# Eight feed-forward projections moved into the last steps of the attention before them, with VectorE as first reader

## The reference, cut to what matters

```python
x = x + tanh(g_xattn[0]) * L0_xattn(ctx_1024, layernorm(x), mask, ...)
x = x + tanh(g_ffn[0]) * L0_ffn(layernorm(x), ...)

def L0_ffn(x):                                  # x: (2048, 128)
    combine = route(x)                          # sigmoid scores of 16 experts in 4 groups,
                                                # best 2 groups, best 4 experts, weights times 2.5
    up = einsum('th,ehi->eti', x, expert_up)    # 16 experts, 64 wide
    down = einsum('eti,eih->eth', silu(up), expert_down)
    moe_out = einsum('te,eth->th', combine, down)
    shared = silu(x @ shared_up) @ shared_down  # 256 wide
    return moe_out + shared
```

## Time and profile before

| | us |
|---|---|
| median of 3 runs (lowest to highest) | 1184.56 (1184.32 to 1186.83) |
| the profiled execution, its own time | 1186.89 |
| its span | 1185.2 |
| TensorE busy (share of the span) | 1099.5 (93%) |
| VectorE busy | 718.4 (61%) |
| ScalarE busy | 706.9 (60%) |
| GpSimd busy | 469.6 (40%) |

### The profile page before, as it was taken

The page is one execution under the profiler, slowest core; times in us unless marked ns, Lnnn a source line. Parts: engine busy times, 40 slices in busy tenths (PEclk is TensorE's granted clock), DMA queues, the critical chain, the costliest instruction groups (busy, mean ns, idle before and its releaser), DMA issues. The chain is left out here.

```text
span 1185.2 us, 22867 instructions
## 1 busy us (share of the span) xinstructions
PE 1099.5 (93%) x8921; PEld 792.8 (67%) x8937; DVE 718.4 (61%) x1385; ACT 706.9 (60%) x1290; POOL 469.6 (40%) x741
## 2 busy tenths in 40 slices
PE   5988898899999999999999889988979988999998
PEld 3554268788888888888887556653546663466667
DVE  6762447555566556656565259984558993645554
ACT  4675530466666666666666468886448986644440
POOL 5771001133422233344444363521484534644441
PEclk8897899899999999999999899998989998999999
DMA  9200000100000000000000200000000000033320
GB/s 334 91 2 1 0 1 2 71 2 1 2 2 1 1 2 1 1 2 1 1 2 1 54 1 2 2 2 0 1 1 1 2 2 1 11 96 103 99 74 19
DMA packets 13884, 29.42 MB, mean 25 GB/s; under 512 B 2737, under 2 KB 5073, under 8 KB 13010
## 3 DMA queue, kind: packets, MB, share of 16 engines
q1 hardware_dynamic: 13778, 27.96, 7.2%
HBM read 25.14 MB, written 1.25 MB: 22 GB/s over the span
## 5 line engine op out<-in xcount | busy, mean ns | idle before, releaser
L1321 POOL TENSOR_TENSOR work<-work 128x1024 f32<-128x1024 f32 x64 | 121.3, 1896 | 268.3 <-DVE work L1415 268.3
L1402 DVE TENSOR_REDUCE work<-psum 128x8 f32<-128x1024 f32 x64 | 78.1, 1220 | 86.4 <-PE psum L1201 86.4
L1343 ACT ACTIVATE work<-work 128x1024 f32<-128x1024 f32 x64 | 67.4, 1053 | 95.8 <-DVE work L1406 95.8
L1413 DVE TENSOR_REDUCE work<-work 128x8 f32<-128x1024 f32 x64 | 77.4, 1209 | 71.9 <-ACT work L1343 71.9
L1772 PEld LDWEIGHTS psum<-w_down,work 128*128 128x128 f32 x768 | 99.1, 192 | 27.1 <-issue 25.6
L1772 PE MATMUL psum<-w_down,work 128*128 128x128 f32 x768 | 100.2, 275 | 1.1 <-DVE x L1892 0.7
L1098 DVE TENSOR_REDUCE work<-psum 128x8 f32<-128x1024 f32 x64 | 75.4, 1220 | 23.9 <-PE psum L853 23.6
L1046 ACT ACTIVATE work<-psum 128x512 f32<-128x512 f32 x128 | 74.2, 598 | 21.4 <-PE psum L867 20.5
L867 PEld LDWEIGHTS psum<-ident,work 128*128 128x128 f32 x512 | 57.2, 142 | 40.5 <-issue 21.7
L1406 DVE TENSOR_TENSOR work<-psum,work 128x1024 f32<-128x1024 f32 x64 | 78.4, 1225 | 6.4
L867 PE MATMUL psum<-ident,work 128*128 128x128 f32 x512 | 76.3, 280 | 5.4 <-ACT work L1046 3.6
(11 more groups left out here) (344 smaller groups left out, 2482.0 us busy)
## 6 DMA issues: line engine op xcount, KB each, us to landing
work<-chosen SPq DMA_DIRECT2D x80, 128.0 KB, 2.9
x<-in_x SPq DMA_DIRECT2D x2, 512.0 KB, 5.3
ctx_tok<-in_ctx SPq DMA_DIRECT2D x2, 512.0 KB, 6.6
xnt<-in_xt SPq DMA_DIRECT2D x1, 1024.0 KB, 9.0
ctxt<-in_ctxt SPq DMA_DIRECT2D x1, 1024.0 KB, 10.9
mask<-in_mask SPq DMA_DIRECT2D x1, 1024.0 KB, 10.1
w_down<-in_down SPq DMA_DIRECT2D x1, 1024.0 KB, 8.0
ctx_tok<-in_g SPq DMA_DIRECT2D x1, 1024.0 KB, 4.9
```

The source lines that it names most:

```text
L1321: pool.tensor_tensor(prob[:, u % 2, h, :], prob[:, u % 2, h, :], rinv[:, u % 2, h].unsqueeze(2).broadcast_to([P, 8, P]), ALU.mult)\
L1343: act.activation(p, p, ACT.Exp).then_inc(S["exp"], 1)
L1402: dve.tensor_reduce(nmax[:, u % 2, h], s, AX.X, ALU.max, negate=True).then_inc(S["max"], 1)
L1413: dve.tensor_reduce(rsum[:, u % 2, h], prob[:, u % 2, h, :], AX.X, ALU.add).then_inc(S["sum"], 1)
```

## The change

The generator of the attention calls two functions of the following stage (`up` and a new `put_by`). `up(0)` to `up(7)` are issued by TensorE in steps 16 to 22, between the output projection and the score of the step; VectorE copies each result from PSUM into the ring as it is, at the end of its own step; ScalarE applies Silu in place, in the ring, for these eight, after `activate(23)` and before `r.keep(act, 0)`. The yields move from step 21 behind step 22, so the prelude (now units 8 to 12 and the three score matmuls) stands directly in front of the attention's last turn. The scaling of the last pair moves from ScalarE to VectorE. `head` goes from 6 to 13; `ahead` stays 24.

```diff
+    def scale_last(self, dve, n):
+        S = self.S
+        dve.wait_ge(S["root"], n + 1)
+        dve.wait_ge(S["turned"], n - 1)
+        dve.wait_ge(S["normed"], n)
+        for i in range(self.per):
+            b = n * self.per + i
+            ins = dve.tensor_scalar(self.xn[:, n % 2, i * P:(i + 1) * P], self.k.x[:, b * P:(b + 1) * P],
+                                    self.r[:, b:b + 1], self.nm[:, b:b + 1], ALU.mult, ALU.add)
+        ins.then_inc(S["normed"], 1)
...
-    STEPS, LAST = NB + 7, NB + 5
+    STEPS = NB + 7
+    EARLY = {16: (0,), 17: (1,), 18: (2,), 19: (3,), 20: (4,), 21: (5, 6), 22: (7,)}
...
         for s in range(STEPS):
-            if s == LAST:
-                yield
...
             if s < NB:
                 project(s)
+            for n in EARLY.get(s, ()):
+                if n == 0:
+                    pe.wait_ge(S["put"], NB)
+                k.made[1].early_up(pe, n)
             if 0 <= s - 4 < NB:
                 score(s - 4)
...
+        yield
         after.turn(pe, NB // 2 - 1)
...
-            if s == LAST:
-                yield
...
-        after.scale(act, NB // 2 - 1)
+        yield
         after.keep(act, NB // 2 - 1)
...
+            for n in EARLY.get(s, ()):
+                if n == 4:
+                    dve.wait_ge(S["pv"], 12)
+                k.made[1].put_by(dve, n)
+        after.scale_last(dve, NB // 2 - 1)
         yield
...
     def wait_ready(eng, n):
 
-        eng.wait_ge(S["prod"] if second else S["act"], n + 1)
+        if n < early:
+            eng.wait_ge(S["early"], n + 1)
+        else:
+            eng.wait_ge(S["prod"] if second else S["act"], n - early + 1)
...
+    def up(pe, n):
+        g, j = divmod(n, J)
+        tokens = slice(g * GT, (g + 1) * GT)
+        if early and n == 0:
+            pe.wait_ge(k.late[0], k.late_count[0])
+        if prev and j == 0:
+            prev.ready(pe, g)
+        if B <= n < B + early:
+            pe.wait_ge(S["raw"], n - B + 1)
+        elif n >= B:
+            pe.wait_ge(S["act"], n - B - early + 1)
+        pe.matmul(up_banks[n % B][:, :], tiles[j][0], k.xnt[:, tokens], start=True, stop=True)\
+          .then_inc(S["up"], 1)
...
+    def put_by(dve, n):
+
+        dve.wait_ge(S["up"], n + 1)
+        dve.tensor_copy(ring[n], up_banks[n % B][:, :]).then_inc(S["raw"], 1)
...
-        for n in range(head):
-            up(n)
+        for n in range(early, head):
+            up(pe, n)
...
-        for n in range(head):
+        for n in range(early, head):
             activate(n)
         yield
...
             activate(n)
+        for n in range(early):
+            j = n % J
+            act.wait_ge(S["raw"], n + 1)
+            act.activation(ring[n], ring[n], function, bias=tiles[j][1] if tiles[j][1] is not None else 0.0)\
+               .then_inc(S["early"], 1)
         if routed:
             r.keep(act, 0)
...
-                                head=6, spare=(k.ctx_tok, *k.big, k.negb),
+                                head=13, early=8, spare=(k.ctx_tok, *k.big, k.negb),
```

More of the change, by code:

```diff
@@ L102, in stages @@
             made.append(make(made[-1] if made else None))
+        self.made = made
         with self.nc.Block() as block:
@@ L189, with __init__ @@
 class Stage:
-    def __init__(self, tensor, scalar, vector, gpsimd, sync, ready, added=None, over=None):
+    def __init__(self, tensor, scalar, vector, gpsimd, sync, ready, added=None, over=None, early_up=None, put_by=None):
         self.tensor, self.scalar, self.vector, self.gpsimd, self.sync = tensor, scalar, vector, gpsimd, sync
         self.ready, self.added, self.over = ready, added, over
+        self.early_up, self.put_by = early_up, put_by
 def in_turn(programs):
@@ L1644, in feed_forward @@
 def feed_forward(k, prev, tag, sub, tiles, function, ahead, lags, one_down=False, routing=None, spare=(), bias=None,
-                 requantise=None, joint=False, on_act=False, head=None):
+                 requantise=None, joint=False, on_act=False, head=None, early=0):
     nc, bank = k.nc, k.bank
@@ L1676, in feed_forward @@
     assert last_sub or a.at <= TAIL_AT, a.at
-    names = ["up", "act", "down", "added"]
+    names = ["up", "raw", "early", "act", "down", "added"]
     names += ["up2", "second", "prod"] if second else []
@@ L1722, in feed_forward @@
     roots = [(0, NG - 1), (NG - 1, NG)] if joint else [(g, g + 1) for g in range(NG)]
-    def tensor(pe):
[L1725 to L1738, removed]
+    def up(pe, n):
[11 more added lines that the diff above has]
+          .then_inc(S["up"], 1)
+        if second:
+            if n >= 2:
+                pe.wait_ge(S["second"], n - 1)
+            pe.matmul(bank[2 + n % 2][:, :], tiles[j][2], k.xnt[:, tokens], start=True, stop=True)\
+              .then_inc(S["up2"], 1)
+    def put_by(dve, n):
+        dve.wait_ge(S["up"], n + 1)
+        dve.tensor_copy(ring[n], up_banks[n % B][:, :]).then_inc(S["raw"], 1)
+    def tensor(pe):
         def select(n):
@@ L1804, in tensor @@
             if m + ahead < N:
-                up(m + ahead)
+                up(pe, m + ahead)
             if m < N:
@@ L2029, in over @@
         eng.wait_ge(S["down"], DOWNS)
-    return Stage(tensor, scalar, vector, gpsimd, sync, ready, all_added, over)
+    return Stage(tensor, scalar, vector, gpsimd, sync, ready, all_added, over, up, put_by)
 class Requantise:
```

## The result

| | us |
|---|---|
| after, median of 4 runs (lowest to highest) | 1175.46 (1175.15 to 1175.90) |
| before, on the same chip, 4 runs | 1184.44 (1183.88 to 1186.83) |
| ratio, 95% interval | 0.992 (0.9902 to 0.9939) |
| forecast | 1178.4 (1174.0 to 1183.0) |
| profiled execution after: own time, span | 1175.18, 1173.5 |

The change saves 9.0 us, 6.2 were forecast. First the windows of the changed kernel, cut at its own steps: each attention step from 16 to 20, step 21 with the rest of the drain, units 8 to 12 with the scores, the way to the choice, the choice, and then the stretch behind the keep. The columns are those of the earlier trace rows.

What follows compares the result with a forecast made beforehand. Bound: waits between engines in the drain, the prelude blocking it, a serial last pair, and a keep delayed by 17 projections. Terms -8.1 + 1.0 + 0.9 + 1.8 - 2.3 - 2.1 + 2.5, recorded as -6.2: 1178.4 us (1174.0 to 1183.0).

Steps and rivals of the forecast that it cites:

- The prelude in the way: Feed-forward prelude before step 21: moved out of the way, step 21 starts at about 105.7 instead of 113.84, -8.1 us.
- Units 0 to 4 free: Steps 16 to 20: early projections of 0.92 us each fill TensorE's waits, hidden by the exponential on ScalarE, cost 0.
- Clock in the drain: Attention's last steps: clock effect of one projection more per step uncertain, taken as +1.0 us (bounds -1.2 and +4.5).
- Rival A: Clock holds everywhere, 0.5 gained in the drain, no fall behind the choice: -10.3 us, 1174.3 us; chance 0.10.
- B: Drain projections not free, low clock through steps 18 to 21, +4.5 instead of +1.0: -2.7, 1181.9 us; chance 0.15.
- D: Steps 16 to 20: early projections hold TensorE, copies on the exponential's path, 3.5 us more: -2.7, 1181.9 us; chance 0.05.
- Units 5 and 6, and 7 to 12: Units 5, 6 in step 21 before gather(15): +0.9 us; units 7 to 12 and scores before the last turn: +1.8.
- rival C: Between out(15) and last turn: six projections at half clock, turn 13.3 us after out(15), +5.6, 1190.2 us; chance 0.07.
- Scaling on VectorE "gives nothing": Last pair's scaling moved to VectorE: 0.56 us for 0.88, under cover of the projections, so no gain; without cover -0.3.
- Last turn to choice, choice to keep: Last turn to choice at full clock: -2.3 us; choice to keep with ten projections left, VectorE the bound: -2.1 us.
- New idle time: TensorE idle 4.6 us in the choice before the keep; clock falls, half-speed work behind it: +2.5 us (lower bound 0).
- The two clock terms: Clock in the drain, taken as +1.0 us, and fall of the clock from TensorE's new idle time, taken as +2.5.

Runs made afterwards that it cites:

- the spread alone: Changed kernel, head still 13, four of the eight in-place Silus moved into the prelude and four behind units 13, 16, 19 and 22: 1175.18 us, ratio 0.9915.
- The version with both halves: Changed kernel with head=10 and in-place Silus spread, four in the prelude, four behind units 13, 16, 19, 22: 1171.32 us, on another chip 1173.10 us.
- the copies doubled: Changed kernel with one more VectorE read of the same bank (512-column maximum) before each of the eight raw copies: 1176.50 us, ratio 0.9932.
- head 10: Changed kernel with head=10 instead of 13, units 10 to 12 moved from before the last turn to behind the choice: 1177.67 us, ratio 0.9931.

## Why the prediction was right, and which terms were off

**The prelude in the way: right.** Step 21 now begins at 103.03, when pair 5 is kept (0.56 us of wait for L368). The kernel with the yields moved and nothing early shows the block's removal by itself (-7.8 us, where -8.1 was forecast).

**Units 0 to 4 free: right.** Step lengths of 3.89 and 5.07 us with a projection in them, against 3.90 and 5.20 without. The copy that had no row takes

```profile
82.62 0.67 DVE L1772 COPY ctx_tok<-psum 128x512 f32<-128x512 f32 x1
```

0.67 us, where I took 0.69 between 0.2 and 0.69. The estimate of 0.66 us by the Trainium skill, "VectorE: DVE Perf Modes", section on the TRN2 errata, for one column per cycle agrees; the two-fold mode (0.39) is not seen. The scaling from SBUF took 0.30 us for 128 columns, where the same table's estimate with the two-fold mode is 0.13; whether the mode or the fixed part is the reason, one size can't tell. Doubling the read moved nothing in these steps.

**Clock in the drain: wrong in sign.** "I take +1.0 (bounds -1.2 and +4.5)" was the step that failed. The clock was 1.00 through all of it, and the stretch is 1.3 us shorter than 8.1 explains, 1.2 of it in one step (5.10 us at 0.50, 3.88 now). I had reasoned that a level seen as low before would stay low and then double the projections; but the added work changed the level. The kernel with five unread projections shows that by itself in its trace, and ten profiles with such projections against two without agree; in the median the effect of that kernel (1.4 us) is not clear of noise. Rival A had this half of the answer; B and D, which made these steps longer, fall with it.

**Units 5 and 6, and 7 to 12: right**, +0.89 and +1.73 for +0.9 and +1.8. The last turn waited for TensorE's queue as foreseen, and with it rival C falls: 7.18 us from out(15) to the turn, not 13.3.

**Scaling on VectorE "gives nothing": wrong.** It was priced as 0.56 us for 0.88 under cover. Undoing it costs 5.0 us, because ScalarE's table load and five Silus are then queued behind the wait for the root. The sum came out right all the same, since it was made for the version that has it; the sentence about what the move is worth was not.

**Last turn to choice, choice to keep: right.** -2.46 for -2.3, -2.12 for -2.1. The choice is bound by VectorE, 14.40 us as forecast, and ScalarE's Silus in place (2.17 and 2.18 us for four each, 4.25 from first to last, near the lower end of 4.2 to 4.8 for eight) end when that chain does. The keep stands on both; with three projections more behind the choice it stood on ScalarE.

**New idle time: mechanism right, size off.** I took +2.5; it was +1.50 in the profile, and +1.44 by the kernel that fills it. I had the clock fall some 2 us into the idle time; it fell only at its end (with 4.15 us of idle time, not 4.6), and the low stretch is short:

```profile
132.40:135.90 3.50, 3.13 (x7) 1.68 (x9) 0.36 (x2) 1.97 (x4) 0.00 (x0) 0.51 0.02 5
```

About 3.4 us at the low level, not the 4 to 7 that I had derived from the longer low stretches of the earlier trace rows, of which a part was idle anyway. The median puts it at 2.7 us (1175.46 against 1172.74), across two sets of timings.

**The sum.** The terms as recorded add up to -6.3, not -6.2; that moves the forecast by 0.1 us. The two clock terms, 2.3 and 1.0 us, make up 3.3 of the 3.6 us between -6.3 and -9.90 in the profiles. Both erred on the same side, so the measured 1175.46 lies nearer to rival A's 1174.3 than to the forecast's 1178.4: of A, the drain came true and the full clock behind the keep did not. The medians differ by 9.0: before's profiled execution lay 2.45 us above its median of 1184.44, after's 0.28 below. How the median's share is split between clock and the rest in steps 16 to 20 stays open; the split in the table is that of one execution each.

## What to carry to other kernels

A wait of the busiest engine is a place for later work, and that work can do two things: it fills the wait, and it can keep the engine's clock up through the stretch, as in the ten profiles here. So price it with the level at both ends, and do not carry over the level that the emptier stretch had. When an operation is moved from one engine to another, do not compare durations: look at what is queued behind it on the engine that it leaves, a table load above all. And after each such move ask again which of the engines sets the next hand-over; here fewer units ahead of the turn cost 2 us alone, the spread alone changed nothing, and together they gained 4.3 us on one chip and, against the spread alone, 2.1 on another.

## What the runs showed that I had not expected

- With one unread projection per step the clock was 1.00 where it had been 0.50 and 0.80, in a drain where TensorE had been busy 2.97 of 3.90 us and 3.77 of 5.20. It is no guarantee for what follows: with the scaling back on ScalarE the clock fell as step 21 began.
- The times of one kernel spread, by and large with its mean clock. Before, 21 runs on one chip lie 6.3 us apart; the changed kernel's lie 0.75 and 2.5 us apart, and with the idle time filled 1.1. The version with both halves has two groups of times, at 0.972 to 0.974 and at 0.977 to 0.978, some 3.5 us apart, and two runs of 1168.56 and 1168.78 at 0.981. Part of such differences lies far from the change. The profiles of the changed kernel and of its repeat are of the same code; over 200 to 235 us the first has a low stretch and the second none:

```profile
200.00:235.00 35.00, 29.94 (x264) 25.43 (x263) 19.35 (x30) 18.15 (x28) 9.63 (x10) 0.90 0.16 61
200.00:235.00 35.00, 29.63 (x283) 25.05 (x282) 20.11 (x31) 17.93 (x28) 9.63 (x10) 1.00 0.16 61
```

- An idle time of 4.15 us took the clock down only as it ended. In three more profiles with the same idle time (4.15, 4.16 and 4.15 us: the scaling on ScalarE, the repeat, the copies doubled) and in one with 3.91 (the spread alone) it fell 0.4 to 1.0 us behind the end. A wait of 3.89 us for ScalarE (scaling on ScalarE) ended with 0.98 over its 112 to 116 and 0.71 behind it, while one split into 1.41 and 2.85 us (head 10) ended in 0.50 over 134.5 to 141. Behind 0.72, 1.25 and 1.24 us it did not fall.
